# A two-layer attention, FP4 and routed-expert kernel: eight slots for target rows, and four transfers moved to other queues and steps

## The chip, the cores and the metric

The kernel runs on one core of one Trainium2 chip. The metric is the device time of one execution in microseconds (us), as a median of several executions. The core has five engines that follow their own instruction streams: TensorE (PE, with its weight loads as PEld), VectorE (DVE), ScalarE (ACT), GpSimd (POOL) and SyncE (SP). They meet only at semaphores. Transfers are issued by SP, ACT or POOL and run on the core's 16 DMA engines.

## The reference: what is computed

The input is 8 rows of 512 tokens with 128 features, in float32. Two layers are applied. The second one is what matters here:

```
xn = layernorm(x)
q = (xn @ Wq + bq) as 16 heads of 64;  k = xn @ Wk + bk;  v = xn @ Wv + bv   # one k and v for all heads
attn = softmax(q @ k.T / 8) @ v, all heads side by side, @ Wo + bo
p = softmax(xn @ Wg + bg); the two best of 8 experts per token, weights renormed
ffn = sum over the two: weight * (gelu(xn @ W1[e] + b1[e]) @ W2[e] + b2[e])
x = x + attn + ffn
```

The first layer (an attention without softmax whose projections are small MLPs, and an FP4-quantised gated FFN) is computed in the same manner row by row.

## The kernel before

**Rows and steps.** The work is written as one list of steps, and every engine walks through that list in its own stream. A row `r` (0 to 7) has 64 attention steps `k` = 0 to 63: a step is one 128x512 block of scores (`first`, L1395 and L1396: two matmuls), its exponential on ACT (L821), and after each four steps the products with the values (`values`, L1423 and L1434). Eight steps are one pair of heads. The first layer of the next rows is spread over the same steps.

**Row maxima.** For every head, PE multiplies q by k once more (`mx`, L1351), DVE takes maxima (L990), and at `k % 8 == 5` PE transposes the maxima of the next pair of heads (`mt`, L1356) and ACT copies them to `mrow` (`copy_m`, L768). In the same step ACT then rounds a new q (`round_q`, L762), which waits for three matmuls of PE. `store_m` (L486 to L490) copies `mrow` with a transfer into one partition row of `q_lm`, where `first` of the next pair reads it, three steps later (at `k % 8 == 0`). `store_m` is issued by SP. PE waits for it on `m_loaded`.

**Softmax sums.** SP also carries the sums through memory and back: at `k` = 12 of a pair a store of `sraw` (L508), for each second pair a load of `sums` that waits for two such stores (L514), five steps later a store of the inverses (L519) that SP waits for, and four broadcast loads of them (L495). For the last two pairs of row 6, the steps fall at `k` = 4 and `k` = 9 of row 7.

**Experts.** Tokens are scattered by POOL to zones of memory by expert. In row 7, after `k` = 15, 23 and 31, come 8, 8 and 7 tiles of 512 tokens (`INSERT`), 23 in all. A tile has four steps `m` = 0 to 3 ("ye"): `first` (three matmuls), gelu on ACT twice (L826), a subtraction on DVE (`part_l`, L1225), and three steps later `second` (three matmuls, L1259 to L1261). Counting steps in fours, a block `here` has steps `c` = 0 to 3, and a tile is one block. At `c` = 1, `tile_events` puts two things in one step: the turn of the rows of the next tile (`tx`: four transposes of PE, then DVE's `tile_in`), and the turn of the output of the tile two blocks back (`ty`: four transposes, then DVE's copy to `y_m` in `tile_turned`). POOL then scatters the output with four indirect transfers (L701).

**Target rows.** `tile_in` computes where a tile's rows go (`to_f`, `to_u`). `to_u` has `WT` = 4 slots, so DVE first waits until the scatters of the tile four before have landed:

```
if t >= WT:
    landed(dve, t - WT)
```

`y_m` has three slots (`YM`), with a wait of the same kind for the tile three before.

**Loads of row 7 by SP.** At `k` = 0 SP loads the weights of tiles 0 to 3, 1 MB each, one after the other (`load_tile_weights`, L534 to L537, with two values read from the table first). At `k` = 9 it loads the rows of tiles 0 and 1 (`load_tile_rows`, L547, with one value read first). The first `tx` is at `k` = 13. Later weights follow when a tile's output has been taken, and later rows two tiles ahead. At `k` = 41 (`LANDED_AT`) SP waits for the last scatters and loads all landed rows, eight times 512 KB (`load_landed`, L554), over the place of the expert weights. DVE adds them to the result from `k` = 46 (`combine`, L1143), two steps for each row.

Of the kernel before, what the change touches and what calls it, by code (L numbers as in the profile page):

```python
# [24 lines left out]
F32 = mybir.dt.float32  # L25
F32R = mybir.dt.float32r
U32 = mybir.dt.uint32
# [4 lines left out]
P = 128  # L32
# [40 lines left out]
def two_layers(nc, a, out):  # L73
# [31 lines left out]
    TILE = 32  # L105
    SMALL = 4
    OUTB = 2
    WT, XT, YT, YM = 4, 2, 2, 3

    INSERT = {15: 8, 23: 8, 31: 7}  # L110
    assert sum(INSERT.values()) == TILES
# [19 lines left out]
    GATE_CUTS = [52, 53, 55, 56]  # L131
    SLOT_CUTS = [59, 60, 61]
    TABLE_CUTS = [61, 62, 62, 63]
    LANDED_AT = 41
    COMBINE_AT = [46 + 2 * n for n in range(NB)]
    SPLIT_STEPS = [6 + 3 * j for j in range(2 * E)]

# [54 lines left out]
        return past.t if past is not None and past.kind == "ye" and past.m == HC - 1 else None  # L192

    def tile_events(st):
        if st.g is None or st.g % TT != 1:
            return []
        here = st.g // TT
        return [(use, tile_of[i]) for use, i in (("tx", here + 1), ("ty", here - 2)) if i in tile_of]

    def row_steps(st):  # L200

# [91 lines left out]
    with ctx:  # L293
# [78 lines left out]
        w_t = nc.alloc_sbuf_tensor_at("w_t", [P, WT, 4, HID], F32R, offset=tile_base)  # L372
        yab = nc.alloc_sbuf_tensor_at("yab", [P, NB, TT, 2, P], F32, offset=tile_base)
        b_t = sb("b_t", [P, WT, 8])
        to_f, to_u = sb("to_f", [P, TT]), sb("to_u", [P, WT, TT], U32)
        zeros = part_h[:].rearrange("p n s -> p (n s)")[:, 0:TT * ROW].bitcast(F32)

        bank = [ctx.enter_context(nc.psum_tensor(f"bank{i}", [P, S], F32)) for i in range(8)]
# [25 lines left out]
        table_set, tile_hi = sem("table_set"), sem("tile_hi")  # L404
        wt_loaded = [sem(f"wt_loaded{i}") for i in range(WT)]
        xm_loaded = [sem(f"xm_loaded{i}") for i in range(XT)]
        to_set, y_scattered = sem("to_set"), [sem(f"y_scattered{i}") for i in range(WT)]
        yab_loaded = [sem(f"yab_loaded{i}") for i in range(NB)]
        resident, out_ready, stored = sem("resident"), sem("out_ready"), sem("stored")
        x1_done, x0_done, xq_done, hq_done = sem("x1_done"), sem("x0_done"), sem("xq_done"), sem("hq_done")  # L410
# [30 lines left out]

        def landed(eng, t):

            eng.wait_ge(y_scattered[t % WT], TT * (t // WT + 1) * 16)

        block = ctx.enter_context(nc.Block())

# [1 line left out]
        def _(sp):  # L449
# [32 lines left out]
            def store_expert(e):  # L482
                sp.wait_ge(expert_l, 2 * e + 2)
                sp.dma_start(w_rows[e], w_t[:, e % WT, :, :].bitcast(F32)).then_inc(w_stored[e % WT], 16)

            def store_m(gp_):  # L486
                read_out(sp, ("mt", gp_))
                at_ = (2 * gp_) % HEADS
                sp.dma_start(q_lm[DK:DK + 1, at_:at_ + 2, :].bitcast(F32), mrow[:, gp_ % 2, :].bitcast(F32))\
                  .then_inc(m_loaded[gp_ % 2], 16)  # L490

            def load_inverse(pair):
                sp.wait_ge(normed, max(pair - 1, 0))
# [53 lines left out]
                sp.dma_start(x_m[:, t % XT, :, :], x_rows[bass.ds(row, S), :].rearrange("(p i) c -> p i c", p=P))\  # L547
                  .then_inc(xm_loaded[t % XT], 16)

            def load_landed(n):  # L550
                if n == 0:
                    for t in range(TILES - WT, TILES):
                        landed(sp, t)
                sp.dma_start(yab[:, n], y_rows[1 + 2 * S * n:1 + 2 * S * (n + 1), :]  # L554
                             .rearrange("(i p b) d -> p i b d", p=P, b=2)).then_inc(yab_loaded[n], 16)

            def store_out(n):
                if n < NB - 1:
                    sp.wait_ge(out_ready, n + 1)
# [2 lines left out]
                sp.dma_start(out[n].rearrange("(i p) d -> p i d", p=P), xres[:, n, :, :]).then_inc(stored, 16)  # L562

            for st in steps:
                for event in head_events(st):
                    if event[0] == "mt":
                        store_m(event[1])
                for r, k in row_steps(st):
                    sums_and_inverses(r, k)
                if st.kind in ("pre", "o") and st.k == X_LOAD_AT and 0 <= st.r + 2 < NB:  # L570
                    sp.wait_ge(x1_done, st.r + 2)
                    load_x(st.r + 2)
                if st.kind == "o" and st.r == 0:
                    for j, k in enumerate(SPLIT_STEPS):
                        if st.k == k - 4:
                            stage_expert(j)
                        if st.k == k + 2 and j % 2:
                            store_expert(j // 2)
                if st.kind in ("o", "ye") and st.r == NB - 1:
                    if st.kind == "o" and st.k == 0:  # L580
                        for i in range(WT):
                            sp.wait_ge(w_stored[i], E // WT * 16)
                        for t in range(WT):
                            load_tile_weights(t)
                    if st.kind == "o" and st.k == 9:
                        for t in range(XT):
                            load_tile_rows(t)
                    here, c = divmod(st.g, TT)
                    if c == 2:
                        t = tile_of.get(here + 1, -1) + XT  # L590
                        if XT <= t < TILES:
                            load_tile_rows(t)
                    if c == 0:
                        t = tile_of.get(here - 2, -1) + WT
                        if WT <= t < TILES:
                            load_tile_weights(t)
                    if st.kind == "o":
                        for n in range(NB):
                            if st.k == LANDED_AT:
                                load_landed(n)  # L600
                            if st.k == COMBINE_AT[n] + 2 and n < NB - 1:
                                store_out(n)
            store_out(NB - 1)
# [3 lines left out]
        def _(pool):  # L607
# [89 lines left out]
            for t in range(TILES):  # L697
                read_out(pool, ("ty", t))
                pool.wait_ge(to_set, t + 1)
                for i in range(TT):  # L700
                    pool.indirect_dma_start(y_rows, bass.IndirectOffsetOnAxis(ap=to_u[:, t % WT, i:i + 1], axis=0),  # L701
                                            y_m[:, t % YM, i, :], None).then_inc(y_scattered[t % WT], 16)

        @block.scalar
        def _(act):
# [59 lines left out]
            def copy_m(pair):  # L765
                ps, free = filled(act, ("mt", pair))
                act.wait_ge(m_loaded[pair % 2], pair // 2 * 16)
                act.activation(mrow[:, pair % 2, :], ps[0:2 * TT, 0:P], ACT.Identity).then_inc(free, 1)  # L768

            def begin(use, n):  # L770
                if use == "xt":
                    ps, _ = filled(act, ("xt", n))
                    act.activation(x_h[:, n % 2, :], ps[:], ACT.Identity).then_inc(xh_done, 1)
                if use == "k":
                    ps, _ = filled(act, ("k", n))
                    act.activation(k_hl[:, n % 2, :], ps[:], ACT.Identity, bias=bk[:, 0:1])
                    act.activation(k_h1[0:DK, n % 2, :], ps[0:DK, :], ACT.Identity, bias=bk[0:DK, 0:1]).then_inc(k_rounded, 1)
# [36 lines left out]
            for st in steps:  # L814
# [13 lines left out]
                for event in head_events(st):  # L828
                    if event[0] == "q":
                        round_q(event[1])  # L830
                    elif event[0] == "mt":
                        copy_m(event[1])
                for _, n, s in l0_events(st):
                    l0(n, s)
                for use, n in begin_events(st):
# [18 lines left out]
        def _(dve):  # L854
# [246 lines left out]
            def tile_in(t):  # L1101
                i = t % 2
                ps, free = full(("tx", t))
                dve.tensor_copy(xt_h[:, i, :], ps[:]).then_inc(tile_hi, 1)
                dve.wait_ge(tile_hi, t + 1)
                dve.tensor_tensor(xt_l[:, i, :], ps[:], xt_h[:, i, :].bitcast(F32), ALU.subtract).then_inc(free, 1)
                if t >= WT:
                    landed(dve, t - WT)
                target = x_m[:, t % XT, :, P]
                link(dve.scalar_tensor_tensor(to_f[:], target, 0.0, spare[:, t, :], ALU.is_equal, ALU.mult))  # L1110
                dve.tensor_tensor(to_u[:, t % WT, :], to_f[:], target, ALU.add).then_inc(to_set, 1)

            def tile_turned(t):
                ps, free = full(("ty", t))
# [428 lines left out]
```

## Time and profile before

| what | value |
|---|---|
| median of 3 runs | 1462.54 us (1460.64 to 1464.7) |
| the profiled execution, its own time | 1460.9 us |
| span of the profiled execution | 1459.0 us |
| PE, DVE, ACT, POOL busy | 1300.1, 1013.9, 708.1, 252.5 us |
| mean granted clock of TensorE | 0.953 |
| bytes moved | 100.26 MB |

Times in a trace are microseconds from the start of the span. "Busy" is the time in which an engine executed; matmuls overlap, so that two rows of the timeline can overlap too. Idle time before an instruction is given with what ended it. A granted clock of 1.00 is the higher of TensorE's two levels, 0.50 the lower.

### The profile page before, as it was taken

How to read it: one execution, taken by the hardware profiler on the slowest of the kernel's cores; microseconds unless marked ns; L12 is line 12 of the kernel's file. 1: busy time of each engine (PE TensorE's matmuls, PEld its weight loads, DVE VectorE, ACT ScalarE, POOL GpSimd, SP SyncE). 2: the span in 40 equal slices, each digit the busy share in tenths (PEclk: the TensorE clock that was granted, in tenths of full speed). 3: DMA queues.
4: the chain of work that ended last, by engine and by line, in shares of the span. 5: the costliest groups of instructions: out<-in, count | busy, mean ns of one | idle time of the engine just before them, and what ended most of it. 6: DMA issues, size and time to landing. Idle time of an engine off the chain costs nothing.

```text
span 1459.0 us, 22233 instructions
## 1 busy us (share of the span) xinstructions
PE 1300.1 (89%) x7377; PEld 767.7 (53%) x7377; DVE 1013.9 (69%) x2393; ACT 708.1 (49%) x1300; POOL 252.5 (17%) x306
## 2 busy tenths in 40 slices
PE   4569888999999999999999999999998778979877
PEld 2335445555555555555555555555454466656634
DVE  7777776578757875787677767776776456666655
ACT  3136454544454445444545454545454464757531
POOL 3132222201010111011001200110002035242510
PEclk9579999999999999999999999999999899999989
DMA  2042442002000200020002000200003255445242
GB/s 72 14 130 93 128 139 103 31 17 77 24 29 17 82 22 26 17 82 24 24 17 82 26 23 17 82 27 21 16 18 113 78 167 171 135 157 163 72 154 59
DMA packets 72372, 100.26 MB, mean 69 GB/s; under 512 B 29196, under 2 KB 49228, under 8 KB 68292
## 3 DMA queue, kind: packets, MB, share of 16 engines
q1 hardware_dynamic: 59876, 70.69, 15.6%
q0 software_dynamic: 10192, 27.44, 5.8%
q8 instruction: 61, 1.00, 0.3%
q10 hardware_dynamic: 2192, 0.71, 0.2%
q14 instruction: 51, 0.42, 0.1%
HBM read 59.86 MB, written 38.68 MB: 68 GB/s over the span
## 4 chain that ended last, share of the span: by engine, by line
PE 61%; DVE 15%; issue 12%; POOL 6%; DMA 2%; SPq 2%; ACT 1%; DVEq 0%; POOLq 0%; ACTq 0%
PE bank L1423 13%; PE bank L1395 7%; PE bank L1351 6%; PE bank L1396 6%; PE bank L1434 6%; POOL y_rows L701 5%; PE bank L1455 4%; DVE mneg L990 3%; PE bank L1275 3%; PE bank L1259 3%; PE bank L1260 2%; PE bank L1261 2%; PE bank L1310 2%; DVE q_lm L984 2%; PE bank L1292 1%
## 5 line engine op out<-in xcount | busy, mean ns | idle before, releaser
L821 ACT ACTIVATE wide<-bank 128x512 f32<-128x512 f32 x512 | 301.5, 604 | 502.8 <-PE bank L1396 492.5
L990 DVE TENSOR_REDUCE mneg<-bank 128x1 f32<-128x512 f32 x512 | 347.4, 686 | 203.6 <-PE bank L1351 197.7
L1395 PE MATMUL bank<-q_hh,k_hl 128*128 128x512 f32 x512 | 236.2, 461 | 19.8 <-DMA q_lm<-mrow 18.2
L1423 PE MATMUL bank<-wide,v_w 128*32 128x512 f32 x2048 | 248.7, 604 | 0.5 <-issue 0.5
L1351 PE MATMUL bank<-k_hl,q_hh 128*128 128x512 f32 x512 | 208.5, 409 | 36.0 <-DVE mneg L990 22.1
L1396 PE MATMUL bank<-q_lm,k_h 65*128 65x512 f32 x512 | 204.2, 399 | 0.0
L1395 PEld LDWEIGHTS bank<-q_hh,k_hl 128*128 128x128 f32 x512 | 97.7, 191 | 151.6 <-issue 109.4
L1351 PEld LDWEIGHTS bank<-k_hl,q_hh 128*128 128x128 f32 x512 | 98.7, 193 | 73.7 <-issue 52.8
L631 POOL TENSOR_TENSOR rs<-rs,power 128x4 f32<-128x4 f32 x24 | 24.6, 1026 | 626.2 <-DVE rs L892 626.2
L1434 PE MATMUL bank<-wide,ones 128*32 128x512 f32 x992 | 129.1, 592 | 0.0
L701 POOL DMA_INDIRECT y_rows<-y_m,to_u x92 | 92.4, 1004 | 177.0 <-DVE y_m L1117 155.0
L1423 PEld LDWEIGHTS bank<-wide,v_w 128*32 128x32 f32 x2048 | 53.9, 110 | 122.7 <-issue 108.4
L762 ACT ACTIVATE q_hh<-bank,bq 128x512 fp32r<-128x512 f32 x128 | 87.6, 684 | 53.2 <-PE bank L1261 53.2
L984 DVE SCALAR_TENSOR_TENSOR q_lm<-bank,bq,q_hh 64x512 fp32r<-64x512 f32 x128 | 94.7, 740 | 23.7 <-ACT q_hh L762 21.6
L1396 PEld LDWEIGHTS bank<-q_lm,k_h 65*128 65x128 f32 x512 | 98.0, 191 | 10.8 <-issue 2.0
L673 POOL DMA_INDIRECT x_rows<-xr,slot_u x64 | 65.3, 1020 | 219.3 <-DVE slot_u L1063 176.1
L826 ACT ACTIVATE part_h<-bank,b_t 128x512 fp32r<-128x512 f32 x92 | 63.4, 690 | 69.7 <-PE bank L1261 63.5
L1225 DVE TENSOR_TENSOR part_l<-wide,part_h 128x512 fp32r<-128x512 f32 x92 | 61.6, 688 | 28.0 <-ACT wide L826 27.7
L1434 PEld LDWEIGHTS bank<-wide,ones 128*32 128x32 f32 x992 | 32.2, 110 | 74.8 <-issue 74.8
L1455 PE MATMUL bank<-wo,on 128*128 128x128 f32 x512 | 62.7, 282 | 8.7 <-DVE on L1185 4.8
L1259 PE MATMUL bank<-part_h,w_t 128*128 128x512 f32 x92 | 41.3, 449 | 31.6 <-DVE part_l L1225 28.2
L1455 PEld LDWEIGHTS bank<-wo,on 128*128 128x128 f32 x512 | 61.9, 198 | 11.6 <-DVE on L1185 6.2
(230 smaller groups left out, 2001.4 us busy)
## 6 DMA issues: line engine op xcount, KB each, us to landing
w_t<-w_rows SPq DMA_DIRECT2D x23, 1024.0 KB
x_rows<-part_h POOLq DMA_DIRECT2D x65, 258.0 KB, 5.7
inv<-inverse_scratch SPq DMA_DIRECT2D x124, 128.0 KB, 3.0
w_rows<-w_t SPq DMA_DIRECT2D x8, 1024.0 KB, 4.9
x_m<-x_rows SPq DMA_DIRECT2D x23, 258.0 KB
stage<-in_L_ffn_W SPq DMA_DIRECT2D x16, 256.0 KB, 4.8
yab<-y_rows SPq DMA_DIRECT2D x8, 512.0 KB, 7.3
xin<-in_L_attn_x SPq DMA_DIRECT2D x8, 256.0 KB, 4.0
```

The lines of the kernel that those rows point to most:

```text
L701: pool.indirect_dma_start(y_rows, bass.IndirectOffsetOnAxis(ap=to_u[:, t % WT, i:i + 1], axis=0), y_m[:, t % YM, i, :], None).then_inc(y_s ...
L762: act.activation(q_hh[:, gh % HEADS, :], ps[:], ACT.Identity, bias=bq[:, gh % H:gh % H + 1])\
L821: act.activation(wide[:, st.g % WIDE, :], ps, ACT.Exp, scale=SCALE1).then_inc(wide_full, 1)
L984: dve.scalar_tensor_tensor(q_lm[0:DK, i, :], ps[0:DK, :], bq[0:DK, h:h + 1], q_hh[0:DK, i, :].bitcast(F32), ALU.add, ALU.subtract).then_in ...
L990: dve.tensor_reduce(mneg[:, (gh // 2) % 2, col:col + 1], ps[:], X, ALU.max, negate=True)\
L1259: pe.matmul(ps, a_h, b_h, start=start, stop=False)
L1351: into(("mx", gh, j), lambda ps: pe.matmul(ps[:], q_hh[:, gh % HEADS, P * j:P * j + P], k_hl[:, n % 2, :], start=True, stop=True))
L1395: pe.matmul(ps, k_hl[:, n, t], q_hh[:, gh % HEADS, :], start=True, stop=False)
L1396: last = pe.matmul(ps, k_h1[0:DK + 1, n, t], q_lm[0:DK + 1, gh % HEADS, :], start=False, stop=True)
L1423: pe.matmul(ps_out[0][rows, :], v_w[:, n, c, TILE * d:TILE * d + TILE], weights, start=(c == 0), stop=(c == TT - 1))
L1434: last = pe.matmul(ps_out[1][rows, :], ones[:], weights, start=(half == 0), stop=(half == 1))
L1455: last = pe.matmul(ps[:, P * i:P * i + P], on[:, g % (H // 4), P * i:P * i + P], wo[:, g, :], start=(g == pairs.start), stop=(g == pairs.s ...
```

## The change

1. **Slots**: a new constant `TO` = 8 takes the place of `WT` = 4 for `to_u`, for its semaphores `y_scattered` and for the wait in `tile_in`.
2. **Maxima**: `store_m` moves from SP to ACT. ACT issues it in the same step, after `copy_m` and `round_q`.
3. **Landed rows**: the eight loads move from SP's `k` = 41 to POOL, right behind its last scatter, with a wait for the last eight tiles.
4. **Weights and rows of the first tiles**: SP loads the weights of tiles 0 to 3 at `k` = 1, 5, 10 and 13, and the rows of tiles 0 and 1 at `k` = 10.
5. **Turns**: `tx` comes at `c` = 0, `ty` at `c` = 2, and no longer both at `c` = 1. The first `tx` is thus at `k` = 12, the last `ty` at `k` = 38 (before: 37).

```diff
-    WT, XT, YT, YM = 4, 2, 2, 3
+    WT, XT, YT, YM, TO = 4, 2, 2, 3, 8
...
-    LANDED_AT = 41
+    ROWS_AT, WEIGHTS_AT = 10, [1, 5, 10, 13]
...
     def tile_events(st):
-        if st.g is None or st.g % TT != 1:
+        if st.g is None:
             return []
-        here = st.g // TT
-        return [(use, tile_of[i]) for use, i in (("tx", here + 1), ("ty", here - 2)) if i in tile_of]
+        here, c = divmod(st.g, TT)
+        use, i = {0: ("tx", here + 1), 2: ("ty", here - 2)}.get(c, (None, None))
+        return [(use, tile_of[i])] if i in tile_of else []
...
-        to_f, to_u = sb("to_f", [P, TT]), sb("to_u", [P, WT, TT], U32)
+        to_f, to_u = sb("to_f", [P, TT]), sb("to_u", [P, TO, TT], U32)
...
         def landed(eng, t):
-            eng.wait_ge(y_scattered[t % WT], TT * (t // WT + 1) * 16)
+            eng.wait_ge(y_scattered[t % TO], TT * (t // TO + 1) * 16)
...
                     if st.kind == "o" and st.k == 0:
                         for i in range(WT):
                             sp.wait_ge(w_stored[i], E // WT * 16)
-                        for t in range(WT):
-                            load_tile_weights(t)
-                    if st.kind == "o" and st.k == 9:
+                    if st.kind == "o" and st.k in WEIGHTS_AT:
+                        load_tile_weights(WEIGHTS_AT.index(st.k))
+                    if st.kind == "o" and st.k == ROWS_AT:
                         for t in range(XT):
                             load_tile_rows(t)
...
+            for t in range(TILES - TO, TILES):
+                landed(pool, t)
+            for n in range(NB):
+                pool.dma_start(yab[:, n], y_rows[1 + 2 * S * n:1 + 2 * S * (n + 1), :]
+                               .rearrange("(i p b) d -> p i b d", p=P, b=2)).then_inc(yab_loaded[n], 16)
...
+            def store_m(pair):
+                read_out(act, ("mt", pair))
+                at_ = (2 * pair) % HEADS
+                act.dma_start(q_lm[DK:DK + 1, at_:at_ + 2, :].bitcast(F32), mrow[:, pair % 2, :].bitcast(F32))\
+                   .then_inc(m_loaded[pair % 2], 16)
...
                         copy_m(event[1])
+                for event in head_events(st):
+                    if event[0] == "mt":
+                        store_m(event[1])
...
-                if t >= WT:
-                    landed(dve, t - WT)
+                if t >= TO:
+                    landed(dve, t - TO)
```

## Rows read from the trace of the kernel before

**Rows 1.** The page: busy time of each engine, share of the span, instructions

```profile
PE 1300.1 (89%) x7377; PEld 767.7 (53%) x7377; DVE 1013.9 (69%) x2393; ACT 708.1 (49%) x1300; POOL 252.5 (17%) x306
```

**Rows 2.** Waits, whole run: engine, line, for whom: us in total, times, longest

```profile
DVE to_f L1110 <- DMA y_rows<-y_m,to_u: 43.3, 11, 5.1
...
PE bank L1395 <- DMA q_lm<-mrow: 18.2, 2, 11.3
```

**Rows 3.** Timeline, one stalled tile: DVE's wait and POOL's first scatter before it

```profile
1173.22 1.16 POOL L701 DMA_INDIRECT y_rows<-y_m,to_u  x1 [51.43 <-DVE y_m L1117]
...
1182.17 0.16 DVE L1110 SCALAR_TENSOR_TENSOR to_f<-x_m,spare 128x4 f32<-128x4 f32 x1 [3.64 <-DMA y_rows<-y_m,to_u]
```

**Rows 4.** Timeline of PE: turns of outputs (ty) in the three groups of tiles

```profile
1170.39 0.60 PE L1265 MATMUL bank<-ident,y_t 128*128 128x128 f32 x4
...
1176.83 0.60 PE L1265 MATMUL bank<-ident,y_t 128*128 128x128 f32 x4
...
1217.25 0.70 PE L1265 MATMUL bank<-ident,y_t 128*128 128x128 f32 x4
...
1255.34 0.60 PE L1265 MATMUL bank<-ident,y_t 128*128 128x128 f32 x4
...
1302.08 0.66 PE L1265 MATMUL bank<-ident,y_t 128*128 128x128 f32 x4 [0.20 <-DVE y_t L1123]
...
1337.55 0.60 PE L1265 MATMUL bank<-ident,y_t 128*128 128x128 f32 x4
...
1372.39 0.66 PE L1265 MATMUL bank<-ident,y_t 128*128 128x128 f32 x4
```

**Rows 5.** Windows: busy of each engine, granted clock, DMA share, GB/s

```profile
1260.00:1310.00 50.00, 39.08 (x174) 30.59 (x173) 28.48 (x53) 28.33 (x45) 22.81 (x23) 0.93 0.51 165
```

**Rows 6.** Windows: the five microseconds behind PE's longest wait

```profile
1137.00:1142.00 5.00, 4.12 (x11) 2.83 (x11) 1.72 (x4) 1.19 (x2) 0.00 (x0) 0.50 0.02 2
```

**Rows 7.** Timeline of SP's transfers at the start of row 7: start, us to issue

```profile
1119.87 0.37 SPq L534 DMA_DIRECT2D w_t<-w_rows  x1
...
1129.95 0.62 SPq L508 DMA_DIRECT2D sums_scratch<-sraw  x1
...
1135.90 0.72 SPq L489 DMA_DIRECT2D q_lm<-mrow  x1
...
1142.12 2.43 SPq L495 DMA_DIRECT2D inv<-inverse_scratch  x4
1145.79 1.48 SPq L547 DMA_DIRECT2D x_m<-x_rows  x2
```

**Rows 8.** Timeline of PE there: steps 6 and 8, and the first tx

```profile
1124.88 0.50 PE L1395 MATMUL bank<-q_hh,k_hl 128*128 128x512 f32 x1
...
1137.88 0.77 PE L1395 MATMUL bank<-q_hh,k_hl 128*128 128x512 f32 x1 [11.35 <-DMA q_lm<-mrow]
...
1148.86 0.60 PE L1265 MATMUL bank<-ident,x_m 128*128 128x128 f32 x4
```

**Rows 9.** Timeline in row 5: round_q at step 5, and step 8 on PE

```profile
854.60 0.66 ACT L762 ACTIVATE q_hh<-bank,bq 128x512 fp32r<-128x512 f32 x1
...
857.43 0.43 PE L1395 MATMUL bank<-q_hh,k_hl 128*128 128x512 f32 x1
```

**Rows 10.** Timeline of PE, end of row 7: last ty (step 37), steps 38, 46, 48

```profile
1384.69 0.63 PE L1265 MATMUL bank<-ident,y_t 128*128 128x128 f32 x4
...
1387.97 0.50 PE L1395 MATMUL bank<-q_hh,k_hl 128*128 128x512 f32 x1
...
1401.23 0.50 PE L1395 MATMUL bank<-q_hh,k_hl 128*128 128x512 f32 x1
...
1409.70 0.77 PE L1395 MATMUL bank<-q_hh,k_hl 128*128 128x512 f32 x1 [6.82 <-DMA q_lm<-mrow]
```

**Rows 11.** Timeline there: POOL's last scatter of four begins; SP's loads of landed rows

```profile
1386.33 0.96 POOL L701 DMA_INDIRECT y_rows<-y_m,to_u  x1 [0.77 <-DVE y_m L1117]
...
1395.57 7.23 SPq L554 DMA_DIRECT2D yab<-y_rows  x8
```

More of the change, by code:

```diff
@@ L406, in two_layers @@
         xm_loaded = [sem(f"xm_loaded{i}") for i in range(XT)]
-        to_set, y_scattered = sem("to_set"), [sem(f"y_scattered{i}") for i in range(WT)]
+        to_set, y_scattered = sem("to_set"), [sem(f"y_scattered{i}") for i in range(TO)]
         yab_loaded = [sem(f"yab_loaded{i}") for i in range(NB)]
@@ L484, in store_expert @@
                 sp.dma_start(w_rows[e], w_t[:, e % WT, :, :].bitcast(F32)).then_inc(w_stored[e % WT], 16)
[L486 to L490, printed above, removed]
             def load_inverse(pair):
@@ L548, in load_tile_rows @@
                   .then_inc(xm_loaded[t % XT], 16)
[L550 to L555, printed above, removed]
             def store_out(n):
@@ L564, in _ @@
             for st in steps:
-                for event in head_events(st):
-                    if event[0] == "mt":
-                        store_m(event[1])
                 for r, k in row_steps(st):
@@ L598, in _ @@
                         for n in range(NB):
-                            if st.k == LANDED_AT:
-                                load_landed(n)
                             if st.k == COMBINE_AT[n] + 2 and n < NB - 1:
@@ L700, in _ @@
                 for i in range(TT):
-                    pool.indirect_dma_start(y_rows, bass.IndirectOffsetOnAxis(ap=to_u[:, t % WT, i:i + 1], axis=0),
-                                            y_m[:, t % YM, i, :], None).then_inc(y_scattered[t % WT], 16)
+                    pool.indirect_dma_start(y_rows, bass.IndirectOffsetOnAxis(ap=to_u[:, t % TO, i:i + 1], axis=0),
+                                            y_m[:, t % YM, i, :], None).then_inc(y_scattered[t % TO], 16)
+            for t in range(TILES - TO, TILES):
[3 more added lines that the diff above has]
+                               .rearrange("(i p b) d -> p i b d", p=P, b=2)).then_inc(yab_loaded[n], 16)
         @block.scalar
@@ L1106, in tile_in @@
                 dve.tensor_tensor(xt_l[:, i, :], ps[:], xt_h[:, i, :].bitcast(F32), ALU.subtract).then_inc(free, 1)
-                if t >= WT:
-                    landed(dve, t - WT)
+                if t >= TO:
+                    landed(dve, t - TO)
                 target = x_m[:, t % XT, :, P]
                 link(dve.scalar_tensor_tensor(to_f[:], target, 0.0, spare[:, t, :], ALU.is_equal, ALU.mult))
-                dve.tensor_tensor(to_u[:, t % WT, :], to_f[:], target, ALU.add).then_inc(to_set, 1)
+                dve.tensor_tensor(to_u[:, t % TO, :], to_f[:], target, ALU.add).then_inc(to_set, 1)
             def tile_turned(t):
```

## The prediction

> **What bounds the kernel now.** I read the page first, then the waits, then the timeline of row 7. TensorE is busy nine tenths of the span [rows 1], so only an edit that lets PE run on can pay. Rows 0 to 6 hold no wait that the change touches. The waits that it does touch are two [rows 2]: VectorE waited 43.3 us, 11 times, for scatters of outputs to land, and PE waited 18.2 us, twice in 64 pairs of heads, for the row of maxima. All 13 lie in row 7. What is to be seen in the timelines is that each of them ends in an idle PE, and a PE at its lower clock level behind it.
>
> **Eight slots (edit 1).** In the stalled tile POOL begins its scatter at 1173.22, and DVE is let go at 1182.17 [rows 3]: 9.0 us for four scatters and their landing. DVE stands in `tile_in` of tile t for tile t-4. Behind that wait in its stream comes `tile_turned` of tile t-3, which POOL's next scatter needs. So a tile can't take less than 9.0 us plus DVE's copy and the handovers, some 10.3 us, and behind DVE stands `part_l`, for which PE's `second` waits. With eight slots tile t asks for tile t-8, which landed long before. The wait that is left (`YM`, three tiles back) asks 9.0 us and about 1 us more over three tiles, 3.4 us a tile. PE is next, and a tile without the stall shows its price: from 1170.39 to 1176.83, 6.44 us [rows 4]. From the first to the last `ty` that the stalls touch, the three groups of tiles took 46.86, 46.74 and 34.84 us for 5, 5 and 4 blocks [rows 4]. At 6.44 us a block they take 32.2, 32.2 and 25.8: 14.7 + 14.5 + 9.1 = **38.3 us gained**. This holds the clock that PE gets back (0.93 in the stalled middle, [rows 5]). DVE was busy 28.5 of 50 us for about 4.9 tiles [rows 5], 5.8 us a tile, so it fits in 6.44, but narrowly. The DMA engines: share 0.51 of 50 us, 5.2 us a tile. At 6.44 us that is a share of 0.81. I take it as enough; the other end is that they hold a tile at 7.5 us, which costs 14 blocks x 1.06 = 15 us.
>
> **Turns in other steps (edit 5).** The same eight transposes, and the same copies. They spread DVE's work over two steps, which I cost at nothing because PE is the bound in a tile; bounds are 0 and 0.2 us for each of 23 tiles, either way.
>
> **Weights and rows of the first tiles (edit 4), with edit 2.** Before, SP issues four loads of 1 MB from 1119.87 on, a small store behind them at 1129.95, and can send the maxima only at 1135.90 [rows 7]. PE stands 11.35 us, until 1137.88 [rows 8]. With the maxima on ACT's queue and one load at a time this wait goes. What is late next? The first `tx` is now at step 12, and SP reaches its loads of rows only behind steps 4, 5, 9 and 10. I follow SP. The first weights at 1119.9 as before, since the table sets that, issued by 1121.3. The four loads and the small store had landed by 1135.9: at most 4.0 us for 1 MB. So the store of sums behind the first load lands at about 1125.3, the load of sums is issued, and the second weights cost 2.9 us of SP ((1129.95 - 1119.87 - 1.5)/3, values included): 1128.9. The inverses, ready about then from DVE's step 8, go out behind 1 MB: back at 1132.6. Four broadcasts, 2.4 us [rows 7]: 1135.1. The third weights, 2.9: 1138.0. One value, 1.2 us (between 1142.12 + 2.43 and 1145.79): the rows of tile 0 are issued at 1139.3. Before, they had landed within 3.1 us (1145.79 to 1148.86, [rows 7, 8]); now the rest of 1 MB is ahead of them: **1143**, and 1141 to 1147 as bounds. PE is there much sooner: step 6 at 1124.88 [rows 8], four steps at 1.66 us (13.26 us for eight, [rows 10]) and three short ones of 0.7: 1133.6. So PE waits about 9.4 us at `tx`. Before, it was at this place at about 1147.1 (1148.86 less step 13's matmuls). That is 4.1 us gained. The 5 us at a granted clock of 0.50 behind the wait [rows 6] were already inside the 1147.1; they now come behind `tx` and cost 2.2 us again. **1.9 us gained.** The ends are -2 (rows at 1147) and 13.4 (no wait). The cover of this load before was the stall itself: step 9 of SP's stream was free of competing work by the time PE moved on.
>
> **Maxima by ScalarE (edit 2).** ACT issues a transfer of 0.7 us in step 5, behind `round_q`. PE has 24 matmuls of the values ahead of it there, so ACT would wait anyway. The transfer starts later than SP's did, by `round_q`. In the tightest case, step 5 of rows 0 to 6, `round_q` ends at 855.26, and PE wants the row at 857.43 [rows 9]: 2.17 us. The unhindered transfer took 1.98 us from issue to PE (1135.90 to 1137.88, [rows 7, 8]). It just fits; all other pairs have over a microsecond more. I take 0.4 us lost in all. If an ACT issue takes 0.4 us longer than SP's, it is 7 x 0.2 = 1.5 us, and more than that only from the rival below. SP loses an order of 64 issues, which frees it; nobody waited for it in rows 0 to 6.
>
> **Landed rows by GpSimd (edit 3), with edits 2 and 5.** PE's second wait for maxima, 6.82 us until 1409.70 [rows 10], stands behind eight loads of 512 KB that SP issued for 7.2 us [rows 11]. On ACT's queue the row is free of them: 6.8 gained, and 2.2 for the clock as above, 9.0. Against it: the last `ty` was at 1384.69 and now follows step 38's start, 1387.97 + 0.7 [rows 10], 4.0 us later, since the values lie between. `ty` to scatter is 1.6 us [rows 10, 11], scatter to landed 9.0 [rows 3]: 1399.3. Then POOL loads; `combine` of row 0 wants them on DVE behind step 46's maximum, at about 1401.23 + 1.6 = 1402.8. The transfer is bounded by the 2.0 us of a small one and by 7.3 us (1395.57 to 1402.8, when DVE found them there). At 5 us they land at 1404.3. DVE is 1.5 us late, and some of the following additions crowd with maxima: 1.8 us lost. **7.2 us gained**, ends 9 and 0.
>
> The Trainium skill ("DMA: Bandwidth & Descriptors", Issuing engines are not separate DMA queues) says that transfers issued by different engines run on the same 16 DMA engines and interleave, and that spreading them only saves issue time. Read strictly, the maxima would still share those engines with 4 MB of landed rows, and the 9.0 us would shrink to the time that SP was stuck. The trace of before has only one queue at work there, so it can't tell. The skill ("SBUF — State Buffer", the warning about VectorE and GpSimd-issued transfers) also has certain VectorE instructions block GpSimd from writing descriptors. POOL's scatters show nothing of it here: the last one began on time, 0.77 us after it went idle [rows 11].
>
> **Sum.** 38.3 + 1.9 + 7.2 - 0.4 = 47.0 us. The profiled execution's own time is 1460.9 (its span is 1459.0), so 1413.9. It stood 1.6 below the median of 1462.54, so against that: **1415.5 us**.
>
> **Rivals.**
> A. *The transfers become the bound in the tiles.* For it: a share of 0.81 worked out above, with 512-byte scatters among it. Against it: nothing waited for weights or rows in the one tile that ran at 6.44 us. Price 15 us: 1430.
> B. *No wait at the first `tx`.* For it: transfers of different sizes may not wait for each other as I assume. Against it: SP's own issue work alone brings the rows to about 1137. Price: 11.5 more gained, 1404.
> C. *The end gives nothing*: the landed rows come late by GpSimd, or the maxima wait beside them. For it: both skill rules and the later `ty`. Against it: DVE has idle time there to take up a delay. 1422.7.
> D. *Slower.* The maxima come late at every pair. One mechanism: an ACT-issued transfer waits for its turn, or lands slowly. From 2.2 us it costs at step 5 of rows 0 to 6, from 3.4 us at nearly every one of some 56 pairs; with 4.4 us it eats the 47 us (56 x 1.0 less), and beyond that the kernel is slower, 1475 at 4.9 us. Against it: the 1.98 us measured from SP, of a transfer of the same form; for it only that no row shows this transfer from ACT.
>
> **How the numbers follow.** My forecast 0.60, A 0.14, B 0.11, C 0.11, D 0.03, and 0.01 for a mixture that cancels. The forecast's own ends (head -2, m rows 1.5) give 1409 to 1421; B and C lie just outside, A farther out. To leave no more than 2 in 10 out: 1403 to 1431. About 0.3%, 4.4 us, is what a measurement of this kernel can tell from no change. All cases but D are far below that: faster 0.95, within 0.3% 0.02, slower 0.03.
>
> **What the profile after would show.** Right: no DVE wait of `to_f` for `y_rows`; blocks of tiles of 6.4 to 6.6 us; PE waiting at its first transposes of `x_m`, about 9 us, near 1134 to 1143, and no wait at L1395 for `q_lm`; SP's rows of tile 0 issued near 1139; DVE waiting 1 to 3 us for `yab`. Wrong: blocks over 7 us with PE waiting for `w_t` or `x_m` (A), no wait at `tx` (B), PE waiting for `q_lm` at the end (C) or many short waits for it in rows 0 to 6 (D).

## The result, and the profile after

The changed kernel takes **1409.84 us** (median of 4 runs, 1409.01 to 1411.51), the kernel before beside it 1461.59 (4 runs, 1458.53 to 1464.7): a ratio of **0.9647**, 95% interval 0.9624 to 0.967, so it is faster by about 51.7 us. The forecast was 1415.5, with 47.0 us gained. The profiled execution took 1409.84 itself, with a span of 1408.0: 51.1 us less than the profiled execution before.

The page of the changed kernel: span, busy time of each engine, shares of the chain that ended last, and the issue of the landed rows.

```profile
span 1408.0 us, 22235 instructions
...
PE 1286.0 (91%) x7377; PEld 760.0 (54%) x7377; DVE 1011.7 (72%) x2393; ACT 708.6 (50%) x1300; POOL 270.9 (19%) x314
...
PE 73%; DVE 16%; issue 3%; DMA 2%; ACT 2%; SPq 2%; POOL 1%; DVEq 0%; ACTq 0%; POOLq 0%
...
yab<-y_rows POOLq DMA_DIRECT2D x8, 512.0 KB, 9.4
```

The same row of the page before, the chain's shares by engine:

```profile
PE 61%; DVE 15%; issue 12%; POOL 6%; DMA 2%; SPq 2%; ACT 1%; DVEq 0%; POOLq 0%; ACTq 0%
```

TensorE does the same 7377 matmuls [rows 1] in a shorter span. The chain's shares moved with it: issue fell from 12% to 3% and POOL from 6% to 1%. Before, those pieces lay in the tiles, where the chain ran over POOL's scatters and the idle time between them. Now it runs over PE. A share of the chain is not the time that can be saved: these two fell by 14% of the span together, and the kernel by 3.5%.

The waits for transfers that are left in row 7, from the view of the whole run (us in total, times, longest):

```profile
PE bank L1262 <- DMA x_m<-x_rows: 9.4, 1, 9.4
...
DVE on L1182 <- DMA inv<-inverse_scratch: 3.1, 1, 3.1
...
POOL yab L689 <- DMA y_rows<-y_m,to_u: 2.6, 1, 2.6
```

Both waits of [rows 2] are gone from the view: VectorE no longer waits for scatters, and PE no longer for maxima. In their place stands the one that was forecast, 9.4 us at the first transposes of `x_m`. PE's timeline shows it, and then the tiles:

```profile
1140.94 1.11 PE L1262 MATMUL bank<-ident,x_m 128*128 128x128 f32 x4 [9.38 <-DMA x_m<-x_rows]
...
1168.17 0.60 PE L1262 MATMUL bank<-ident,y_t 128*128 128x128 f32 x4
...
1171.38 0.60 PE L1262 MATMUL bank<-ident,x_m 128*128 128x128 f32 x4
```

From a `ty` to the next `tx` is half a tile here, 3.21 us; the next `ty` stands at 1174.60, so a block takes 6.43 us. [Rows 4] had 6.44 for the one unstalled tile, and (46.86 - 6.44) / 4 = 10.1 on average for the four behind it.

To see in which steps the time was won, I take from both timelines the start of the first score matmul (L1395 before, L1392 after) of a step of row 7. What the difference grows by between two steps is what was won there:

| row 7, start of step | before less after, us | growth | forecast for the stretch |
|---|---|---|---|
| 0 | 2.1 | 2.1 (rows 0 to 6) | -0.4 |
| 14 | 3.6 | 1.5 | 1.9 |
| 16 (first group of tiles done) | 18.9 | 15.3 | 14.7 |
| 24 (second) | 33.9 | 15.0 | 14.5 |
| 32 (third) | 44.0 | 10.1 | 9.1 |
| 46 | 44.0 | 0.0 | 0 |
| 50 | 53.5 | 9.5 | 9.0 |
| 54 | 50.6 | -2.9 | -1.8 |
| 63 | 50.6 | 0.0 | 0 |

A second profile of the changed kernel (the last experiment below) gives 15.3, 12.7 and 9.6 for the three groups, so the middle one was 2.3 us shorter here by chance.

The windows of the changed kernel for five blocks of tiles, and for the two stretches around steps 50 to 54 (length; busy us of PE, PEld, DVE, ACT, POOL with counts; granted clock; DMA share; GB/s):

```profile
1167.00:1199.10 32.10, 32.10 (x159) 26.40 (x158) 26.29 (x51) 25.74 (x41) 22.19 (x19) 1.00 0.73 240
...
1360.00:1366.00 6.00, 5.77 (x37) 2.41 (x35) 6.00 (x18) 2.88 (x7) 0.00 (x0) 1.00 0.99 375
1366.00:1374.00 8.00, 6.52 (x39) 2.04 (x38) 6.01 (x22) 1.24 (x3) 0.00 (x0) 0.79 0.67 217
```

In the tiles PE is busy throughout, at a granted clock of 1.00, where [rows 5] had 39.08 of 50 us and 0.93. VectorE takes 26.29 / 5 = 5.3 us of a 6.43 us tile (5.8 forecast), and the DMA engines have a share of 0.73 (0.81 forecast), at 240 GB/s in place of 165: both fit. At the end the picture turns: VectorE has no idle time for 6 us beside DMA engines at 0.99, and the granted clock is then 0.79 on average over 8 us, that is, part of them are at the lower level. In the table this is the loss of 2.9 us.

### The profile page after: what moved, and what is told of

Its sections match the earlier page's. It is cut to its first block, busy times and chain, and to the rows that moved or that the text cites. A ratio compares the mean times of both kernels' runs of the same rounds, so it can differ in the third digit from the quotient of the medians.

```text
span 1408.0 us, 22235 instructions
## 1 busy us (share of the span) xinstructions
PE 1286.0 (91%) x7377; PEld 760.0 (54%) x7377; DVE 1011.7 (72%) x2393; ACT 708.6 (50%) x1300; POOL 270.9 (19%) x314
## 4 chain that ended last, share of the span: by engine, by line
PE 73%; DVE 16%; issue 3%; DMA 2%; ACT 2%; SPq 2%; POOL 1%; DVEq 0%; ACTq 0%; POOLq 0%
PE bank L1420 14%; PE bank L1392 8%; PE bank L1348 7%; PE bank L1431 6%; PE bank L1393 6%; PE bank L1256 5%; PE bank L1258 5%; PE bank L1257 5%; PE bank L1452 4%; DVE mneg L987 3%; PE bank L1272 2%; PE bank L1262 2%; DVE q_lm L981 2%; PE bank L1307 2%; PE bank L1289 1%
## 5 line engine op out<-in xcount | busy, mean ns | idle before, releaser
L1392 PE MATMUL bank<-q_hh,k_hl 128*128 128x512 f32 x512 | 234.7, 458 | 1.7 <-ACT wide L815 1.4
L1392 PEld LDWEIGHTS bank<-q_hh,k_hl 128*128 128x128 f32 x512 | 97.0, 189 | 131.1 <-issue 89.5
L1348 PEld LDWEIGHTS bank<-k_hl,q_hh 128*128 128x128 f32 x512 | 98.1, 192 | 72.6 <-issue 51.7
L684 POOL DMA_INDIRECT y_rows<-y_m,to_u x92 | 104.2, 1132 | 127.0 <-DVE y_m L1114 105.1
L1222 DVE TENSOR_TENSOR part_l<-wide,part_h 128x512 fp32r<-128x512 f32 x92 | 62.2, 689 | 35.5 <-ACT wide L820 35.1
L820 ACT ACTIVATE wide<-bank,b_t 128x512 f32<-128x512 f32 x92 | 62.8, 683 | 0.0
```

What stands on the lines that cost most here:

```text
L820: ins = act.activation(dst, ps, ACT.Gelu_apprx_tanh, bias=b_t[:, st.t % WT, st.m:st.m + 1])
L1348: into(("mx", gh, j), lambda ps: pe.matmul(ps[:], q_hh[:, gh % HEADS, P * j:P * j + P], k_hl[:, n % 2, :], start=True, stop=True))
L1392: pe.matmul(ps, k_hl[:, n, t], q_hh[:, gh % HEADS, :], start=True, stop=False)
```

## The experiments

The kernels below were measured in three groups, on three chips, each with the kernel before beside them: medians 1468.28 (13 runs), 1470.01 (9) and 1467.47 (9), where the first comparison had 1461.59. So ratios are compared, and a difference in microseconds is the difference of two ratios times 1468. The changed kernel stands at 0.9647 in the first comparison and at 0.9644 in the repeat below; differences are taken from 0.9644. Two ratios can be told apart when they differ by some 0.003, about 4 us.

### Is it the slots? Four slots under the other edits

```diff
-    WT, XT, YT, YM, TO = 4, 2, 2, 3, 8
+    WT, XT, YT, YM, TO = 4, 2, 2, 3, 4
```

> The changed kernel with four slots for target rows in place of eight, all else as changed. My theory: the slots carry about four fifths of the gain, so VectorE waits again for scatters about 11 times, tiles take 10.3 us, and the time is 36 to 42 us above the changed kernel (1446 to 1452 us). Rival: with the turns in separate steps and the maxima on ScalarE the stall would be weaker; then under 25 us above.

Measured: 1469.68 us (8 runs), ratio 1.0007 (0.9992 to 1.0021). That is 53 us over the changed kernel, more than either theory gave; all of the gain is gone. The wait is back and larger than in [rows 2]:

```profile
DVE to_f L1107 <- DMA y_rows<-y_m,to_u: 58.1, 11, 6.0
```

VectorE's timeline of this kernel in two stalled tiles, and behind it that of the kernel before:

```profile
1180.97 0.16 DVE L1107 SCALAR_TENSOR_TENSOR to_f<-x_m,spare 128x4 f32<-128x4 f32 x1 [5.61 <-DMA y_rows<-y_m,to_u]
...
1181.25 1.28 DVE L1222 TENSOR_TENSOR part_l<-wide,part_h 128x512 fp32r<-128x512 f32 x2
1182.45 0.69 DVE L1114 COPY y_m<-bank 128x512 f32<-128x512 f32 x1
...
1192.21 0.16 DVE L1107 SCALAR_TENSOR_TENSOR to_f<-x_m,spare 128x4 f32<-128x4 f32 x1 [5.03 <-DMA y_rows<-y_m,to_u]
```

```profile
1182.45 0.68 DVE L1117 COPY y_m<-bank 128x512 f32<-128x512 f32 x1
...
1192.43 0.16 DVE L1110 SCALAR_TENSOR_TENSOR to_f<-x_m,spare 128x4 f32<-128x4 f32 x1 [4.92 <-DMA y_rows<-y_m,to_u]
```

The loop is 1192.21 - 1180.97 = 11.2 us, and 1192.43 - 1182.17 = 10.3 in the kernel before [rows 3]. The two lines between show why: with the turns in other steps the copy of `y_m`, which POOL's next scatter needs, stands behind two `part_l` (1.28 us) after the wait, where before it came at once. So without the slots nothing is gained, and the edit of the turns is not a neutral one: with four slots the tiles take about 17 us more than before (241.8 us from step 14 to step 32, 224.3 before). That all of this comes from the turns is read from the timeline; the two kernels also differ in edits 2 to 4.

### The slots alone

The kernel before with this and the same change at the other places that use `to_u` and `y_scattered`:

```diff
-    WT, XT, YT, YM = 4, 2, 2, 3
+    WT, XT, YT, YM, TO = 4, 2, 2, 3, 8
...
-                if t >= WT:
-                    landed(dve, t - WT)
+                if t >= TO:
+                    landed(dve, t - TO)
```

> The kernel before with eight slots for target rows and nothing else. My theory: the stall of the tiles goes, 34 to 39 us below the kernel before (ratio 0.974 to 0.977); the two waits for maxima stay. Rival: the whole gain is this edit, because undoing it in the changed kernel cost all of it; then 0.967 or less.

Measured: 1432.29 us, ratio 0.9761 (0.974 to 0.9783): 35.1 us less than before, as expected. Edit 1 gives about two thirds of the whole. In its profile the three groups of tiles (from the first score matmul of steps 15, 23 and 31 to that of the next step) take 155.2 us in all, 193.9 before: 38.7 us won with nothing but the slots changed. Both waits for maxima are still there, and something else:

```profile
PE bank L1395 <- DMA q_lm<-mrow: 17.3, 2, 12.0
...
ACT wide L821 <- remote: 7.4, 1, 7.4
```

The second line is a halt for which the trace knows no releaser. It comes up again in the next experiment.

### The turns together again

```diff
-        here, c = divmod(st.g, TT)
-        use, i = {0: ("tx", here + 1), 2: ("ty", here - 2)}.get(c, (None, None))
-        return [(use, tile_of[i])] if i in tile_of else []
+        here = st.g // TT
+        return [(use, tile_of[i]) for use, i in (("tx", here + 1), ("ty", here - 2)) if i in tile_of]
```

Steps other than those with `st.g % TT == 1` have no turns then, as before.

> The changed kernel with both turns of a tile in its step 1 again. My theory: with eight slots the place of the turns is nearly free; the first tile's turn comes a step later, so the wait there is 1 to 2 us shorter, tiles are 0 to 0.1 us slower each, and the time is within 2.5 us of the changed kernel. Rival: two turns in one step make VectorE late for its subtraction; then tiles of 6.7 us or more and 5 us or more above.

Measured: 1425.64 us, ratio 0.9695 (0.9668 to 0.9722), 7 us over the changed kernel. I ran it again beside other kernels:

> Both turns in step 1 again, a second time. One profile showed tiles 0.2 us slower each (4.6 us in all), the first tile's wait 1.3 us shorter, and a halt of about 7 us at steps 38 to 46 that nothing in the change explains. Theory: the halt is an accident of that execution or is in every run of this kernel; if an accident, 3 to 4 us above the changed kernel; if in every run, 8 us or more above and the same halt in this profile.

Measured: 1427.95 us, ratio 0.9734 (0.9711 to 0.9756), 13 us over it. So the forecast's "nothing" for edit 5 is refuted, and its size is 7 to 13 us. The 13 is the comparison with the changed kernel measured beside it.

Two things are seen in both profiles. The first is not what the expectation above took it for. The tiles are not slower: the three groups take 154.7 and 154.8 us, 153.5 in the changed kernel and 156.4 in its repeat. The time is lost in the attention steps between the groups, nearly all of it in the two steps right behind a group:

| us | before | slots alone | turns together, twice | changed kernel, twice |
|---|---|---|---|---|
| step 16, start to start | 1.40 | 2.66 | 2.77, 2.64 | 1.40, 1.40 |
| step 24, start to start | 1.40 | 2.57 | 2.73, 2.57 | 1.40, 1.40 |
| steps 16 to 22 and 24 to 30, in all | 29.6 | 32.7 | 33.1, 33.0 | 29.6, 29.6 |

The kernel before has the turns together too and loses nothing there: only turns together and eight slots cost these 3.1 to 3.5 us. The second thing is that near step 40 ScalarE and VectorE stand together. Timeline of the first of the two kernels there:

```profile
1349.68 0.39 PE L1347 MATMUL bank<-k_hl,q_hh 128*128 128x512 f32 x1
...
1353.77 1.08 ACT L814 ACTIVATE wide<-bank 128x512 f32<-128x512 f32 x2 [8.28 <-remote]
...
1353.80 1.29 DVE L986 TENSOR_REDUCE mneg<-bank 128x1 f32<-128x512 f32 x2 [6.66 <-remote]
...
1354.42 0.79 PE L1391 MATMUL bank<-q_hh,k_hl 128*128 128x512 f32 x1 [4.34 <-ACT wide L814]
```

PE's records end at 1350.1, yet both readers of its banks begin only at 1353.8. PE's own next matmul waits for them, and takes 0.79 us in place of 0.50; the granted clock is 0.50 from 1354 to 1358. All three profiles of kernels with eight slots and the turns together (this one, its repeat and the slots alone) have the halt once, and no kernel with the turns apart has it. The ends of matmuls are modelled in these records, so it may be PE itself that was held. What holds them isn't shown by any record, and stays open. Two things narrow it. The DMA engines are busy for a share of 0.15 in it, so it isn't a lack of bandwidth. And ScalarE goes on 0.16 us (0.19 in the repeat) before POOL's wait for the last scatters ends (1353.93 and 1355.93), so it may hang on those scatters; no run tests it.

### The maxima by SP again

```diff
             for st in steps:
+                for event in head_events(st):
+                    if event[0] == "mt":
+                        store_m(event[1])
```

The lines stand in SP's block, and are gone from ScalarE's.

> The changed kernel with the maxima's transfer issued by SyncE again. My theory: what blocked them before was four megabytes of weights at once and the landed rows in SyncE's own stream; both are gone from there now. So at step 8 of row 7 TensorE waits 1 to 4 us (SyncE is busy with the sums and one load), at the end of the kernel not at all, and the time is 1 to 4 us above the changed kernel. Rival: the move to ScalarE is itself what removed the 18 us of waits; then 13 us or more above.

Measured: 1418.3 us, ratio 0.9654 (0.963 to 0.9679): 1.5 us over the changed kernel, inside what was expected and not to be told from no difference. Its wait for maxima, at step 8:

```profile
PE bank L1398 <- DMA q_lm<-mrow: 1.6, 1, 1.6
```

With the landed rows on POOL's queue, SP is free at the end and sends the maxima in time. At the head the first `tx` waits 7.8 us in place of 9.4, so a later PE mostly shortens that wait.

### The landed rows by SP again

```diff
                         for n in range(NB):
+                            if st.k == 41:
+                                load_landed(n)
```

The loads stand in SP's block, as before (`load_landed`), and are gone from POOL's.

> The changed kernel with the landed rows loaded by SyncE at step 41 again, maxima still by ScalarE. My theory: the wait for maxima at the end went because they left SyncE's stream, whoever loads the landed rows; within 1.5 us of the changed kernel. Rival: loading by GpSimd matters by itself, because SyncE is held for 7 us and the sums behind it come late: 4 us or more above.

Measured: 1415.0 us, ratio 0.9641 (0.9618 to 0.9664): the same as the changed kernel, as expected. The end of this kernel shows why, and what a queue of one's own is worth. SP's loads, ScalarE's store of the maxima, and PE's matmul that needs them:

```profile
1357.40 6.99 SPq L549 DMA_DIRECT2D yab<-y_rows  x8
1359.40 0.66 ACTq L765 DMA_DIRECT2D q_lm<-mrow  x1
1364.75 0.47 PE L1396 MATMUL bank<-q_hh,k_hl 128*128 128x512 f32 x1 [1.09 <-DMA q_lm<-mrow]
```

ScalarE issues in the middle of SP's eight. PE has the maxima 5.4 us after their issue, which costs it 1.09.

One thing does change. From step 53 to 54, where the changed kernel loses 2.9 us, this kernel takes 4.95 us like the one before (4.77), against 7.69 and 7.63 in the two profiles of the changed kernel. In all five kernels whose landed rows SP loads this stretch takes 4.8 to 5.0 us; in six of the eight where GpSimd loads them and the additions begin at step 46 it takes 5.9 to 9.2. So the loss comes mostly with edit 3, and without that edit is paid elsewhere: here PE's wait for maxima is 1.09 us where the changed kernel has none.

### Both by SP again

```diff
             for st in steps:
+                for event in head_events(st):
+                    if event[0] == "mt":
+                        store_m(event[1])
...
                         for n in range(NB):
+                            if st.k == 41:
+                                load_landed(n)
```

Both stand in SP's block again, and are gone from ScalarE's and POOL's.

> The changed kernel with both the maxima's transfer and the loads of landed rows issued by SyncE again, as before; slots, turns and the first loads as changed. My theory: either of the two moves alone removes the wait at the end, so with both undone it is back: TensorE waits 6 to 8 us for maxima at step 48 of row 7, and the time is 7 to 11 us above the changed kernel, where each alone was within 1 us. Rival: the wait at the end went with the slots or the turns; then within 3 us.

Measured: 1426.63 us, ratio 0.9696 (0.967 to 0.9722): 7.6 us over the changed kernel, as expected. PE's wait is back in its timeline, and SP's shows what held the maxima:

```profile
1376.41 0.76 PE L1402 MATMUL bank<-q_hh,k_hl 128*128 128x512 f32 x1 [7.76 <-DMA q_lm<-mrow]
```

```profile
1362.52 6.97 SPq L555 DMA_DIRECT2D yab<-y_rows  x8
...
1369.60 1.08 SPq L509 DMA_DIRECT2D sums_scratch<-sraw  x1
1370.73 0.69 SPq L490 DMA_DIRECT2D q_lm<-mrow  x1
```

Either edit alone removes the wait at the end or nearly all of it (undoing one of them costs 1.5 and -0.4 us); only undoing both brings it back. They are substitutes, and their gains don't add.

### The weights all at step 0

```diff
-    ROWS_AT, WEIGHTS_AT = 10, [1, 5, 10, 13]
+    ROWS_AT, WEIGHTS_AT = 10, 0
...
-                    if st.kind == "o" and st.k in WEIGHTS_AT:
-                        load_tile_weights(WEIGHTS_AT.index(st.k))
+                    if st.kind == "o" and st.k == WEIGHTS_AT:
+                        for t in range(WT):
+                            load_tile_weights(t)
```

> The changed kernel with the weights of tiles 0 to 3 loaded at step 0 of row 7, one after the other as before, rows at step 10, maxima by ScalarE. My theory: maxima no longer stand behind them, but the softmax sums do: VectorE waits about 10 us for sums at step 8, TensorE runs out behind it, and the rows of tile 0 land 2 to 5 us later; 2 to 5 us above the changed kernel. Rival: with maxima off SyncE's stream the spreading is needless or even harmful, since the rows no longer stand behind a megabyte: equal or faster.

Measured: 1418.82 us, ratio 0.9658 (0.9629 to 0.9688): 2 us over the changed kernel, as expected in size, but less than what two ratios can tell apart. Its waits:

```profile
DVE sums L1169 <- DMA sums<-sums_scratch: 10.7, 1, 10.7
...
PE bank L1349 <- DVE mneg L988: 6.4, 1, 6.4
...
PE bank L1263 <- DMA x_m<-x_rows: 6.5, 1, 6.5
```

VectorE waits 10.7 us for a small load behind 4 MB, and through `mneg` PE waits 6.4. At the first `tx` PE then waits 6.5 us in place of 9.4, so only a part of it comes back.

### The rows of the first tiles early

```diff
-    ROWS_AT, WEIGHTS_AT = 10, [1, 5, 10, 13]
+    ROWS_AT, WEIGHTS_AT = 4, [1, 10, 11, 13]
```

> The changed kernel with the rows of tiles 0 and 1 loaded at step 4 of row 7, and the weights at steps 1, 10, 11 and 13. My theory: the 9.4 us wait at the first transposes of a tile is SyncE's order alone, so it goes and with it most of the lower clock behind it: 9 to 12 us below the changed kernel (about 1399 us). Rival: the wait is bandwidth, or another one (inverses, weights of tile 1) takes its place: under 5 us below.

Measured: 1402.37 us, ratio 0.9556 (0.9538 to 0.9574): 13 us under the changed kernel, somewhat more than expected. PE's timeline has the first `tx` without a wait, and one short wait at a later tile:

```profile
1131.13 0.60 PE L1262 MATMUL bank<-ident,x_m 128*128 128x128 f32 x4
...
1147.30 0.66 PE L1262 MATMUL bank<-ident,x_m 128*128 128x128 f32 x4 [0.80 <-DMA x_m<-x_rows]
```

SP's timeline shows the order that does it:

```profile
1117.07 0.26 SPq L529 DMA_DIRECT2D w_t<-w_rows  x1
...
1125.41 1.47 SPq L542 DMA_DIRECT2D x_m<-x_rows  x2
1126.99 0.36 SPq L514 DMA_DIRECT2D inverse_scratch<-sums  x1
1130.73 2.42 SPq L490 DMA_DIRECT2D inv<-inverse_scratch  x4
```

In the changed kernel the same two loads of rows stand behind the inverses and the third weights, at 1137.03. So the 9.4 us came from the place in SP's queue, as the prediction read it. Most of the rest of the 13 is the clock: behind the wait the changed kernel's next score matmul takes 0.78 us (1141.71) at a granted clock of 0.50 from 1141 to 1146, and here, where PE didn't stand idle, 0.47 (1131.49) at 1.00. By step 14 this kernel is 12.0 us ahead of the changed one, counted from the start of row 7.

### Early rows with later combines, and with landed rows by SP

```diff
-    ROWS_AT, WEIGHTS_AT = 10, [1, 5, 10, 13]
+    ROWS_AT, WEIGHTS_AT = 4, [1, 10, 11, 13]
-    COMBINE_AT = [46 + 2 * n for n in range(NB)]
+    COMBINE_AT = [48 + 2 * n for n in range(NB)]
```

> Rows of tiles 0 and 1 loaded at step 4 (weights at 1, 10, 11, 13), and the additions of landed rows two steps later, from step 48. My theory: VectorE's crowding between steps 46 and 53 costs TensorE a wait for maxima and a stretch at the lower clock, 2.9 us in the changed kernel; two steps later there is less of it: 1 to 3 us below the kernel with early rows alone. Rival: the additions then run into the reciprocals at the very end: equal or slower.

Measured: 1403.05 us, ratio 0.9542 (0.9518 to 0.9565). Not to be told from early rows alone. From step 53 to 54 it takes 4.8 us, where early rows alone take 5.3 and the changed kernel 7.7; but steps 58 to 63 take 9.5 us in place of 7.8. The crowding moved.

```diff
-    ROWS_AT, WEIGHTS_AT = 10, [1, 5, 10, 13]
+    ROWS_AT, WEIGHTS_AT = 4, [1, 10, 11, 13]
...
+                            if st.k == 41:
+                                load_landed(n)
```

The loads of landed rows are gone from POOL's block.

> Rows of tiles 0 and 1 at step 4, weights at 1, 10, 11 and 13, and landed rows loaded by SyncE again. From the runs apart (0.9556 for early rows; 0.9641 against 0.9647 for SyncE's loads): 12 to 15 us below the changed kernel, within 2 us of early rows alone. Rival: SyncE's later weights now collide with its landed rows: over 3 us worse than early rows alone.

Measured: 1403.09 us, ratio 0.956 (0.9542 to 0.9578). The same again. The best versions are these three, at 0.954 to 0.956.

### The changed kernel again

No edit.

> The changed kernel itself, unedited, as the yardstick for the others on this chip. Expected: 0.965 of the kernel before, within 0.003; if a chip's own pace moved earlier runs, its ratio stays.

Measured: 1414.92 us (5 runs, 1413.41 to 1417.56), ratio 0.9644 (0.9625 to 0.9664). Its profile stands 2.2 us behind the first one's at step 24 and 3.5 at step 46 with the same kernel, so a difference of 2 to 3 us between single profiles carries nothing by itself.

## Why the prediction was right

**The tiles.** Forecast 38.3 us, measured 40.4 (44.0 - 3.6), and 37.6 by the second profile, so the excess of 2.1 us isn't one of the kernel. The step held in all parts: a loop set by scatter and landing through four slots, PE next at 6.44 us a block (6.43 measured), and the clock coming back. The two experiments on the slots show the cause: four of them bring the wait back, and eight alone win 38.7 us in the tiles. The tile with the price of 6.44 us was the right row to take. One reading was too wide: not each of the waits had the lower clock level behind it. Behind the one of [rows 3] the granted clock was 1.00 (1182 to 1192), behind the next 0.66 (1192 to 1197).

**The head.** Forecast: the maxima's wait goes, and the first `tx` waits 9.4 us; measured 9.38, and 1.5 us gained in place of 1.9. The times of SP's queue that I had worked out against those of the trace (2.1 us earlier, as row 7 begins earlier): rows issued 1139.3 against 1137.03 + 2.1 = 1139.1; PE let go at 1143 against 1140.94 + 2.1 = 1143.0. SP's queue could be followed instruction by instruction; the early rows then took this wait away.

**The end.** Forecast 9.0 - 1.8 = 7.2 us, measured 9.5 - 2.9 = 6.6; undoing edits 2 and 3 together costs 7.6. The size of the gain was right, its ground only in part. I had the maxima free of the landed rows on a queue of their own. They aren't free of them: a store of maxima took 1.98 us until PE ran with nothing beside it [rows 7, 8], 5.4 us when ScalarE issued it into SP's landed rows, and 5.7 us behind them on SP's own queue (1370.73 to 1376.41). In the changed kernel it was issued 1.2 us behind POOL's first load of landed rows, at 1354.59, and PE began step 48 at 1358.87 without a wait, so it took at most 4.3 us there. What the other queue saves is that the issue itself isn't behind 7 us of SP's other issues. The Trainium skill ("DMA: Bandwidth & Descriptors", Issuing engines are not separate DMA queues) says just this, that another issuing engine saves only the time of issuing, which it calls usually small. The numbers agree, only that this time isn't small here: SP is held for 7 us by eight issues.

The loss was right in size and wrong in its step. I had the landed rows 1.5 us late for VectorE. They weren't: the last four scatters took 7.4 us from the first issue to landed and not 9.0, POOL's first load was issued at 1353.44, and `combine` found its rows at 1358.80 without a wait. Timelines of POOL and DVE:

```profile
1346.05 0.97 POOL L684 DMA_INDIRECT y_rows<-y_m,to_u  x1 [2.86 <-DVE y_m L1114]
...
1353.44 3.94 POOL L689 DMA_DIRECT2D yab<-y_rows  x5 [2.60 <-DMA y_rows<-y_m,to_u]
```

```profile
1358.80 1.13 DVE L1140 SCALAR_TENSOR_TENSOR xres<-yab,gate,xres 128x128 f32<-128x128 f32 x4
```

What goes with the 2.9 us is the crowding that I had put second: VectorE has combines and maxima at once, and PE waits for it until 1367.77:

```profile
1367.77 0.27 PE L1353 MATMUL bank<-ident,mneg 128*8 128x128 f32 x1 [1.48 <-DVE mneg L987]
1367.98 2.93 PE L1420 MATMUL bank<-wide,v_w 128*32 128x512 f32 x16
```

The matmuls behind it run longer, 2.93 us for sixteen, where sixteen of the same take 1.92 us at 1360.44 with a granted clock of 1.00. That the loss appears with GpSimd's loads and not with SP's is seen in the runs; by which way those loads bring the crowding about isn't shown.

**The maxima in rows 0 to 6.** Forecast 0.4 us lost. No wait of PE for `q_lm` is in the view after, so nothing was lost. Row 7 even begins 2.1 us earlier; that came in jumps of 1 to 1.5 us in stretches where both kernels have the same waits and differ in the granted clock, and the profiles of the other kernels begin row 7 anywhere from 3.5 us earlier to 2.1 us later than the one before. I don't count it as the change's.

**The turns.** Forecast nothing, because PE is the bound in a tile, with 0.2 us a tile as the bound. For the tiles themselves this held. But in the attention steps right behind the groups, and near step 40, which the prediction didn't look at, edit 5 is worth 7 to 13 us under eight slots: 3.1 to 3.5 us between the groups, the rest from the halt near step 40 on. The prediction came out right all the same, in part by luck: it counted 38.3 us for the slots as if nothing were lost beside them, and it is edit 5, put at nothing, that keeps the loss away.

**The rivals.** A (transfers bound the tiles) fell: blocks of 6.43 us at a DMA share of 0.73. B (no wait at the first `tx`) fell: 9.38 us. Only with another order of SP's loads is the wait gone. C (nothing at the end) fell: 6.6 us, though its ground, transfers that share, was real. D (late maxima at every pair) fell: not one wait. Its price was added up wrongly: 56 pairs x 1.0 us are 56 us and not 47, and at 4.9 us the same steps give 56 x 1.5 = 84 us over the forecast, 1500 and not 1475. At a chance of 0.03 this moves nothing.

**The total.** 51.7 us measured against 47.0. Of the 4.7 us between them 2.1 had been won when row 7 began, which I count as chance, and 2.1 lie in the tiles, which the second profile doesn't confirm. The end of 1409 that the prediction gave to its own case isn't worked out in it.

## What to carry to other kernels

Follow the queue of the issuing engine instruction by instruction, with what lies ahead of a transfer: that gave here a wait to within 0.1 us and the one line worth 13 us more. When a wait for a slot goes, price the loop by what stands behind it on the same engine, and look at the steps beside the loop too, since the same move of the turns cost about 17 us with four slots and saved 7 to 13 with eight. And undo edits in pairs: two of them may remove the same wait, and each alone then looks worth nothing.

## What the runs showed of the hardware that was not expected

- A store of one row of maxima took 1.98 us until PE ran, with nothing beside it; 5.4 us issued by ScalarE into SP's eight loads of 4 MB in all, 5.7 us behind them on SP's queue; and at most 4.3 us issued by ScalarE just behind the first of GpSimd's eight.
- Eight loads of 512 KB held SP's queue for 7.0 to 7.2 us and POOL's for 6.2 (3.94 for five and 2.23 for three).
- ScalarE and VectorE stood together for 6.3 to 8.3 us behind matmuls whose records had ended, in each kernel with eight slots and the turns together, and went on within 0.04 us of each other. Its cause was not found.
